# Wq and Wk of an attention layer: high and low parts alternating element by element in one tile each

## The reference

```
x = _ln(src) * (1.0 + scale) + shift
q = (x @ Wq + bq)          # 512 x 512, then split into 16 heads
k = (x @ Wk + bk)
v = (x @ Wv + bv)
scores = einsum('bhqd,bhkd->bhqk', q / sqrt(32), k) + attention_bias
probs = softmax(where(src_mask, -inf, scores))
x = x + (einsum('bhqk,bhkd->bhqd', probs, v) @ Wo + bo)
h = _ln(x) * g2 + beta2
out = x + _gelu2(h @ W1 + b1) @ W2 + b2
```

## Time and profile before

| | |
|---|---|
| median of three timed runs | 2448.05 us |
| lowest, highest | 2445.57, 2451.18 us |
| span of the profiled execution | 2446.8 us |
| PE busy, PEld busy | 2363.3 us (97%), 2225.6 us (91%) |
| DVE, ACT, POOL busy | 1740.3, 1323.8, 1833.0 us |
| instructions | 61264 |

### The profile page before, as it was taken

One profiled execution on the slowest core, in us unless ns is written; L12 is line 12 of the kernel. 1 busy time (PEld: TensorE's weight loads), 2 busy tenths in 40 slices (PEclk: granted clock), 3 DMA queues, 4 the chain that ended last, 5 costly groups with the idle time before them and its releaser, 6 DMA issues.

```text
span 2446.8 us, 61264 instructions
## 1 busy us (share of the span) xinstructions
PE 2363.3 (97%) x21034; PEld 2225.6 (91%) x21034; DVE 1740.3 (71%) x2864; ACT 1323.8 (54%) x3663; POOL 1833.0 (75%) x1787
## 2 busy tenths in 40 slices
PE   5999999999999999978999999999979999999998
PEld 3888888888888888868999999999979999999998
DVE  5777777777777777676666667675577677676766
ACT  2666666666666666665555555555443334333432
POOL 3777777777777777778777777777897676767775
PEclk9999999999999999999999999999999999999999
DMA  7344444444444444323434343433465555656563
GB/s 241 115 131 139 136 141 140 139 128 126 134 136 140 141 140 145 101 92 118 164 135 162 146 152 146 152 146 147 164 207 174 188 188 181 190 171 192 173 195 125
DMA packets 289442, 372.13 MB, mean 152 GB/s; under 512 B 29072, under 2 KB 203280, under 8 KB 289232
## 3 DMA queue, kind: packets, MB, share of 16 engines
q1 hardware_dynamic: 289232, 369.44, 46.4%
HBM read 251.68 MB, written 117.70 MB: 151 GB/s over the span
## 4 chain that ended last, share of the span: by engine, by line
PE 90%; POOL 3%; DVE 3%; issue 2%; DMA 1%; ACT 1%; SPq 0%; DVEq 0%; POOLq 0%; ACTq 0%
PE up L1601 14%; PE up L1599 14%; PE up L1600 14%; PE psD L956 5%; PE turn L956 5%; PE psD L958 5%; PE psD L957 5%; PE turn L958 5%; PE turn L957 5%; PE psS L985 4%; PE psS L971 3%; PE psC L995 3%; PE turn L1599 2%; PE turn L1600 2%; PE turn L1601 2%
## 5 line engine op out<-in xcount | busy, mean ns | idle before, releaser
L1599 PE MATMUL up<-T,wc 128*128 128x256 f32 x1792 | 512.3, 286 | 14.1 <-DVE gu L1473 7.8
L1601 PE MATMUL up<-T,wc 128*128 128x256 f32 x1792 | 508.5, 284 | 0.0
L1600 PE MATMUL up<-T,wc 128*128 128x256 f32 x1792 | 506.1, 282 | 0.0
L628 POOL TENSOR_TENSOR s<-s,rinv 128x512 f32<-128x512 f32 x254 | 265.0, 1044 | 221.6 <-DVE rinv L823 221.5
L744 ACT ACTIVATE s<-s,nmx 128x128 f32<-128x128 f32 x1024 | 396.2, 394 | 7.4 <-issue 4.3
L1599 PE MATMUL up<-wc,gs 128*128 128x256 f32 x1280 | 360.9, 282 | 2.3 <-DVE gs L1556 2.3
L1600 PE MATMUL up<-wc,gs 128*128 128x256 f32 x1280 | 360.5, 282 | 0.0
L1601 PE MATMUL up<-wc,gs 128*128 128x256 f32 x1280 | 360.4, 282 | 0.0
L1599 PEld LDWEIGHTS up<-T,wc 128*128 128x128 f32 x1792 | 340.1, 190 | 17.9 <-DVE gu L1473 9.0
L688 POOL TENSOR_TENSOR bias<-bias,mneg 128x512 f32<-128x512 f32 x256 | 335.5, 1334 | 11.2 <-DVE mneg L828 11.2
L1600 PEld LDWEIGHTS up<-T,wc 128*128 128x128 f32 x1792 | 341.6, 191 | 0.0
(11 more groups left out here) (221 smaller groups left out, 6964.6 us busy)
## 6 DMA issues: line engine op xcount, KB each, us to landing
bias<-in_bias SPq DMA_DIRECT2D x128, 512.0 KB, 5.4
gated<-gu SPq DMA_DIRECT2D x128, 512.0 KB, 2.6
adab<-ada_rows SPq DMA_DIRECT2D x64, 512.0 KB, 5.4
gbuf<-gated SPq DMA_DIRECT2D x64, 512.0 KB, 3.9
gu<-gated SPq DMA_DIRECT2D x63, 512.0 KB, 3.8
xin<-in_x SPq DMA_DIRECT2D x32, 512.0 KB, 5.0
resid<-rout SPq DMA_DIRECT2D x64, 256.0 KB, 2.0
r<-resid SPq DMA_DIRECT2D x16, 1024.0 KB, 6.1
```

The costliest lines, as they stand in the source:

```text
L628: eng.tensor_tensor(s[:, b, heads, :], s[:, b, heads, :], rinv[:, b, heads].unsqueeze(2).to_broadcast([P, HG, S]), ALU.mult).then_inc(done, 1)
L1599: pe.matmul(out_ap, sh, mh, start=start, stop=False)
L1600: pe.matmul(out_ap, sh, ml, start=False, stop=False)
L1601: return pe.matmul(out_ap, sl, mh, start=False, stop=stop)
```

## The change

One tile per matrix, `wq` and `wk`, of shape `[P, CH, DM, 2]`, takes the place of the two tiles of each. The last index is the part: 0 high, 1 low. The two entries of `w` for Q and K are views of it with a step of two elements (8 bytes). Everything that used the old tiles uses these views: the ACT and DVE and POOL instructions of the setup that write the parts (and the low ones that read the high part) step two elements, and so do the 3072 weight loads of `project_t`, each of them now 128 elements spread over 1,020 bytes in each partition instead of 512 bytes in a row. The moving operands, the layout of V and O, the total memory (the same bytes at the same addresses in all) and the order of the instructions on all five engines stay as they are; no wait is added or removed.

```diff
--- before.py
+++ after.py
@@ -1686,8 +1686,8 @@
 
         turn = [whole.enter_context(nc.psum_tensor(f"turn{i}", [P, CH, P], F32)) for i in range(2)]
 
-        w = at_once(*((f"w{n}_{part}", [P, CH, DM], F32R) for n in "qkv" for part in ("hi", "lo")))
-        w = [w[0:2], w[2:4], w[4:6], wo]
+        wq, wk, *wv = at_once(*((f"w{n}", [P, CH, DM, 2], F32R) for n in "qk"), *((f"wv_{part}", [P, CH, DM], F32R) for part in ("hi", "lo")))
+        w = [*([t[:, :, :, part] for part in range(2)] for t in (wq, wk)), wv, wo]
         r, T0, hTf, b2_bc, p1c, p5c = at_once(("r", [P, 4, DM], F32), ("T0", [P, 2, 7, 2, 2 * P], F32R), eight("hTf"),
                                               ("b2_bc", [P, DM], F32), ("p1c", [P, 2 * P], F32), ("p5c", [P, 2 * P], F32))
         raw2_0, raw2_1, gs0, gbuf0, c1, e2, e4 = at_once(
```

## The result

The changed kernel is slower. Median of four timed runs: 2462.11 us (2457.44 to 2465.09) against 2448.23 us (2445.57 to 2451.18) of the kernel before on the same chip; ratio 1.0058, 95% interval 1.004 to 1.0076, so +10 to +19 us. I had forecast 2448 us and given "same" a chance of 0.67. The time lies in the wider range that I gave (2442 to 2467 us), but above the forecast's own (2444 to 2453 us), and the change that I had put at nothing is a loss.

A forecast was written before the change was run, and what follows sets the result against it. PE's stream was taken as the bound (97% busy, 99.3% in attention). 2446.8 + 0 (weight loads) + 0 (setup writes and reads) = 2446.8 us profiled, 2448 us as a median; own range 2444 to 2453 us, wider 2442 to 2467 us.

The forecast's parts named there:

- the wider range: Whole kernel: 2442 to 2467 us, taking in the forecast and rivals B, C and D, some 0.8 chance; leaves out A.
- What bounds the kernel: Attention: PE busy 99.3% of 978 us, no idle time to cover a longer stream, so lengthening PE's stream lengthens the kernel.
- 3.1: Cadence in project_t: each ns on it was said to be worth 3.1 us of the total.
- I take 0 us: The 3072 weight loads of project_t: stepping two elements costs nothing, within bounds of -5.4 to +333 us.
- the room: project_t: load's own time 109 ns under a 114.5 ns matmul slot, so about 5 ns growth before the stream waits.
- three widths: Load records of 109, 137 and 191 ns at 32, 64 and 128 columns, read as 109 ns for 128 columns.
- The argument for zero: project_t: moving operand already covers 1,024 bytes in 114.5 ns or less, the stepped load 1,020 in 109; cost 0.
- rival A: project_t's 3072 loads: weight side reads a stepped pattern at half rate, +305 to +333 us; full or in part, chance 0.17.
- Rival B: Q and K projections: stepped load contends with the moving operand, +9 to +19 us, 2455 to 2467 us; chance 0.09.
- The 120 ns of the feed part: Contiguous same-shape loads in the feed part run at 0.1206 us against 0.1145, used to size the contention loss.
- C: project_t: psD groups come down to the cadence of turn, -5.4 us, 2442.6 us; chance 0.06.
- D: Setup: stepped writes of Wq and Wk at double cost, +6 us, 2454 us; chance 0.02.

The follow-up runs named there:

- e4: Against the kernel before: all four parts of Wq and Wk alternate in one tile, so loads step four elements (16 bytes); 2801.18 us, ratio 1.1449.
- e5: Against the kernel before: both Wq parts and Wk's high part in one tile, step three elements, Wk's low part dense; 2593.38 us, ratio 1.059.
- e7: Kernel before, dense loads, with each project_t matmul cut into two of 128 moving columns with a load each; 2775.14 us, one run.
- e8: Changed kernel, stepped loads, with each project_t matmul cut into two of 128 moving columns with a load each; 2810.48 us, one run.
- e9: Kernel before with both parts of transposed input xT interleaved, so project_t's moving operands and project_v's loads step two elements; 2792.15 us, ratio 1.1387.
- e6: Kernel before with the parts of cT interleaved, so 768 output-projection loads step two elements under 512 moving columns; 2445.45 us, ratio 0.9995.
- e1: Changed kernel's stepped tiles and setup writes kept, but Q and K weight loads read 128 neighbouring elements; 2448.6 us, ratio 1.0009 to the kernel before.
- e3: Only Wq interleaved, Wk left in two tiles as in the kernel before; 2452.5 us, ratio 1.0034 to the kernel before.
- e12: Kernel before with each Q and K weight load stepping eight elements (32 bytes) over two chunks; 2817.36 us, one run.

## Why the prediction was wrong

**What bounds the kernel: right.** PE's stream in attention has almost no idle time, nothing hid the loss, and each ns on the cadence was worth 2.8 us where 3.1 had been said: 5.3 ns x 2816 = 14.9 us was found. The 3.1 us counted the 256 distances between groups as well.

**"I take 0 us" for the 3072 loads: the step that failed.** The term was worth +14.9 us. It lies between its bounds (-5.4 to +333 us), but two things under the zero were wrong. The first is the room: "a load may grow by about 5 ns, no more, before the stream waits for it". The load grew by 6.1 ns, which by this sentence costs some 1 ns on the cadence, or 3 us; it cost 5.3 ns. The dense load alone took 111.6 ns where three widths had given 109, so against the mean cadence of 114.8 the room was 3.2 ns, and 117.7 - 114.8 = 2.9 ns of the loss follow from that. For the other 2.4 ns (6.8 us) no run has the cause.

The second is the load's growth, put at nothing. The argument for zero was the moving side, which goes over 1,024 bytes in 114.5 ns "or less". It was the right row, read too kindly. Read as a price, it says that an operand of the array covers 64 lines in 114.5 to 118 ns, that is that a stepped load would take 114.5 to 118 ns instead of 109, as long as the whole slot. It takes 117.7. The working for rival A used another rule than the room above, a cadence of the load's time and 5 ns. With it the row gives at least 119.5 ns, +5 ns and some +14 us (2816 x 5 ns), where the runs show 120.1 ns. That this comes so near is in part luck: the two rules contradict each other, and by e4 and e5 (235.3 and 176 ns, two times and one and a half times 117.7) a longer load carries no such 5 ns on top. I had used the row to say that the memory can do it, and not for how long it takes.

**The Trainium skill's rule.** By "SBUF — State Buffer", section "Door 1: The DMA port swizzle", two accesses in a line run at full bandwidth, and I wrote that the sum stays at 0. The measurement decides: it is nearly true of the weight side (117.7 against 111.6 ns, e7 and e8), which for a stream with 2 to 6 ns of room is not free, and not true of the moving side (230 against 114.5 ns, e9). The sentence of the Trainium skill on non-contiguous patterns ("Advanced Engine Details and Errata", section "PSUM Cachelines"), which I had set beside rival A, is written of PSUM, and no run here tests it there; read of the weights, a large loss came at steps three and four, not at two.

**Rival B (a small loss, 0.09 given to it): the right size, another cause.** Its +9 to +19 us is what was measured, 10 to 19 us. It was told as contention with the moving operand; e8 shows that the load is longer by as much with half as many columns moving beside it, and e6 that beside a moving operand that is long enough it costs nothing. Contention isn't ruled out for the 2.4 ns between 117.7 and 120.1. B had also expected records of unchanged length; they grew from 188 to 195 ns. The 120 ns of the feed part, from which I had the size, are not explained by this: the loads there are dense, and the cadence is the same in the kernel after.

**Rival A: the mechanism is real, but begins later.** A load of twice the length appears at step 4, where e4 lost 355 us, somewhat more than the +305 to +333 us of the full price. At step 2 the load is 5% longer, not 100%. The threshold of 5 ns was too wide, as told above.

**C and D.** No group went below its cadence of before. C also rested on a misreading: of the groups that write `psD` only those with `a` = 1 had 118 ns, those with `a` = 3 had 113.5, so the bank written isn't what sets the level, and C was worth half of its 5.4 us. The writes of the setup, in the rows that answer to the earlier trace rows:

```profile
L443 ACT ACTIVATE wk<-raw_k 128x512 fp32r<-128x512 f32 x4 | 2.3, 656 | 3.5 <-DMA raw_k<-in_Wk 3.5
```
```profile
L385 DVE TENSOR_TENSOR wk<-raw_k,wk 128x512 fp32r<-128x512 f32 x4 | 4.7, 1226 | 0.0
...
L385 DVE TENSOR_TENSOR wq<-raw_q,wq 128x512 fp32r<-128x512 f32 x2 | 1.3, 674 | 0.0
```

ACT's instructions rose from 617 to 656 ns (0.16 us for Wk in all; 652 ns in e1), DVE's on Wk from 947 to 1226, those on Wq fell from 912 to 674. In e1, with the same stepped writes, DVE's are at 954:

```profile
L385 DVE TENSOR_TENSOR wk<-raw_k,wk 128x512 fp32r<-128x512 f32 x4 | 3.6, 954 | 0.0
```

So the step doesn't set the DVE figure. What does isn't shown; in e1 the writes of `wv_lo`, which nothing touched, took 788 ns and not 1056. D's double cost didn't come, and 0 was near enough for this term: of the 1.0 us by which the first K matmul is later, 0.8 us are there before any changed instruction (the first is ACT's at 24.04 us), at the first matmul of all, here of before and then of after:

```profile
16.61 0.66 PE L459 MATMUL psT<-ident,gate 128*128 128x128 f32 x2 [16.61 <-DVE gate L517]
```
```profile
17.42 0.66 PE L459 MATMUL psT<-ident,gate 128*128 128x128 f32 x2 [17.42 <-DVE gate L517]
```

**What stays open.** Why a dense load with 256 moving columns has the two levels of 113.5 and 118 ns, and which of them a group takes; in e1, e3 and e6 it differs for groups whose loads are as dense as before, and since each kernel was traced once, it may be the execution as well as the kernel. Why with 256 moving columns the stepped cadence is 120.1 and not the 117.7 of e8: the dense feed part has the same 120.0 ns, and in e8 the groups behind Wo show 120 too, with 128 moving columns, so it may be a third level of this kind and not a meeting of the step with the moving data. And the -3.5 us of the down product. No run was made for these. The kernel before spreads over as much as any of them, from 2438.84 to 2453.55 us in 23 runs.

## What to carry to other kernels

When a stream of matmuls reloads its weights each time, work out the load's own time and the matmul's own time separately, and count the room between them in ns. Here it was 2 to 6 ns, and a layout that made the load 5% longer took all of it. Measure that time with the load as the only bound, as e7 does: here the estimate from three widths of records was 2.6 ns too low, half of the 5 ns of room that it left. In these runs an element step of two on an fp32r weight tile made the load 5% longer, and it was free only under a moving operand that took longer than the load (e6); on the moving operand the same step doubled the time (e9). A busy share that doesn't move says nothing on such a change: count the instructions in a fixed window, or the distance of the starts.

## What the runs showed of the hardware that was not expected

- A stream that waits for weight loads of 128 fp32r columns starts a matmul every 111.6 ns at step 1, 117.7 at step 2, 176 at step 3, 235 at step 4 and 242 at step 8 (e7, e8, e5, e4, e12; the last three under 256 moving columns). That is 1.84 ns per 16-byte line from step 2 to 4, over a floor of 111.6 ns.
- A moving operand of 256 fp32r columns costs 230 ns at step 2 against 113.5 to 118 ns dense (e9): 1.80 ns per line, and 1.77 to 1.84 ns dense. By these numbers the dense moving stream may already run at the line rate of the stepped loads; only one step was tried on this side, so that is not shown.
- At a granted clock of 0.50 a stepped load of two elements costs nothing: 0.2125 us from start to start in both kernels, in one K group each.
- Loads of two elements' step have records of 195 ns against 188, and under 512 moving columns that costs nothing: the starts are 230 ns apart against 233.4 (e6).
